# Gated attention written out straight, with one-piece evictions of the query and key projection and DMAs that place its halves

## The reference, cut to what matters

```
dist = softmax(mean(x @ Wr + br, axis=1))        # a gate picks 4 of 16 heads for each batch entry
_, idx = top_k(dist, 4)
Q, K, V = (x @ Wq + bq), (x @ Wk + bk), (x @ Wv + bv)     # split into heads of 64
Qs, Ks, Vs = gather(Q), gather(K), gather(V)     # only the 4 picked heads
score = softmax(einsum('bhqd,bhkd->bhqk', Qs, Ks) / 8, axis=-1)
O = einsum('bhqk,bhkd->bhqd', score, Vs)
x = x + (O.reshape(b, s, 256) @ Wo + bo)
```

## Time and profile before

| | us |
|---|---|
| median of 3 runs | 757.16 (755.01 to 757.79) |
| the profiled execution's own time | 755.7 |
| its span | 753.6 |
| gated attention, first scores to output projection | 219.0 to 454.7 |
| PE busy in the whole span | 590.0 (78%) |
| DVE busy | 514.2 (68%) |
| ACT busy | 314.8 (42%) |
| POOL busy | 334.3 (44%) |

### The profile page before, as it was taken

The page is one execution under the profiler, slowest core; times in us unless marked ns, Lnnn a source line. Parts: engine busy times, 40 slices in busy tenths (PEclk is TensorE's granted clock), DMA queues, the critical chain, the costliest instruction groups (busy, mean ns, idle before and its releaser), DMA issues. The chain is left out here.

```text
span 753.6 us, 12641 instructions
## 1 busy us (share of the span) xinstructions
PE 590.0 (78%) x3566; PEld 488.8 (65%) x3567; DVE 514.2 (68%) x980; ACT 314.8 (42%) x577; POOL 334.3 (44%) x296
## 2 busy tenths in 40 slices
PE   5588999952588999998998988677203989989985
PEld 4467888851457777776776777347202877867874
DVE  4698888857139888888888876476612556567562
ACT  2144555412158878788787770233101112112120
POOL 4344444534025344444444431134461196599144
PEclk9799999985699999999999999885556999999998
DMA  6121112000210000000000000762426025034000
GB/s 208 29 56 29 30 28 54 3 8 0 85 32 1 1 1 1 2 0 0 0 0 0 0 1 0 271 199 79 199 100 205 15 96 217 14 158 154 28 14 3
DMA packets 21039, 43.76 MB, mean 58 GB/s; under 512 B 2874, under 2 KB 14139, under 8 KB 18954
## 3 DMA queue, kind: packets, MB, share of 16 engines
q1 hardware_dynamic: 17130, 37.06, 14.8%
q0 software_dynamic: 1776, 4.23, 1.6%
q10 hardware_dynamic: 2096, 2.05, 0.9%
HBM read 31.58 MB, written 8.21 MB: 53 GB/s over the span
## 5 line engine op out<-in xcount | busy, mean ns | idle before, releaser
L889 POOL TENSOR_SCALAR h_p<-h_p,h_rs 128x1024 f32<-128x1024 f32 x64 | 72.1, 1127 | 123.1 <-DVE h_rs L1007 120.5
L1016 DVE TENSOR_REDUCE h_nmx<-h_psS 128x1 f32<-128x1024 f32 x64 | 78.0, 1219 | 20.9 <-PE h_psS L1103 20.2
L957 ACT ACTIVATE h_p<-h_psS,h_nmx 128x1024 f32<-128x1024 f32 x64 | 71.7, 1120 | 29.0 <-DVE h_nmx L1016 28.6
L994 DVE TENSOR_TENSOR h_pTl<-h_psT,h_pTh 128x512 fp32r<-128x512 f32 x128 | 81.3, 676 | 2.1 <-ACT h_pTh L932 2.1
L1066 PE MATMUL h_psT<-ident,h_p 128*128 128x128 f32 x512 | 71.6, 277 | 12.5 <-DVE h_pTl L994 12.3
L1066 PEld LDWEIGHTS h_psT<-ident,h_p 128*128 128x128 f32 x512 | 57.3, 140 | 30.9 <-DVE h_pTl L994 17.8
L932 ACT CAST h_pTh<-h_psT 128x512 fp32r<-128x512 f32 x128 | 69.8, 590 | 7.5 <-PE h_psT L1066 6.7
L1077 PE MATMUL h_psO<-h_pTh,h_vs 128*128 128x256 f32 x256 | 68.0, 301 | 4.6 <-DVE h_oT L1001 4.2
L308 POOL TENSOR_TENSOR a_p<-a_p,a_rs 128x616 f32<-128x616 f32 x32 | 39.0, 1219 | 73.4 <-DVE a_rs L355 73.4
L1077 PE MATMUL h_psO<-h_pTl,h_vs 128*128 128x256 f32 x256 | 62.1, 279 | 0.0
L1103 PE MATMUL h_psS<-h_kh,h_qs 128*128 128x512 f32 x128 | 57.0, 446 | 2.8 <-ACT h_p L957 2.4
(11 more groups left out here) (269 smaller groups left out, 1512.7 us busy)
## 6 DMA issues: line engine op xcount, KB each, us to landing
wst<-in_m_w SPq DMA_DIRECT2D x16, 1024.0 KB, 6.1
bias<-in_m_b SPq DMA_DIRECT2D x8, 640.0 KB, 8.2
rows<-c_blank SPq DMA_DIRECT2D x1, 3250.0 KB, 18.6
xg<-rows SPq DMA_DIRECT2D x1, 2990.0 KB, 11.5
a_qs<-a_qhi SPq DMA_DIRECT2D x16, 128.0 KB, 2.3
a_qs<-a_qlo SPq DMA_DIRECT2D x16, 128.0 KB, 2.3
x_all<-in_x SPq DMA_DIRECT2D x2, 768.0 KB, 10.7
whead<-in_f_w ACTq DMA_DIRECT2D x4, 192.0 KB, 3.8
```

The source lines that it names most:

```text
L889: pool.tensor_scalar(pr[:, c % 4], pr[:, c % 4], rs[:, c:c + 1], 0.0, ALU.mult, ALU.add).then_inc(pn_ready, 1)
L957: act.activation(pr[:, c % 4], psS[c % 2][:], ACT.Exp, bias=nmx[:, c:c + 1], scale=1.0, accum_out=sm[:, c:c + 1]).then_inc(exp_done, 1)
L994: vec.tensor_tensor(pTl[c // QP % 2][part], psT[hf][:], pTh[c // QP % 2][part], ALU.subtract).then_inc(pT_lo, 1)
L1016: vec.tensor_reduce(nmx[:, c:c + 1], psS[c % 2][:], AX.X, ALU.max, negate=True).then_inc(max_ready, 1)
```

## The change

- The loop is gone: all 64 units are written out, and `upto` is a plain wait on a constant. No ninth head is prepared.
- The weights of a head are read by PE straight from `whead`; POOL scales the query part of four heads at once (`scale_q(b)`), before the first unit.
- ACT evicts a projection in one instruction of 128 partitions into a new tile `hi`, and DVE forms the low part in one instruction into `lo`. Six DMAs of 64 x 512 from SP put the halves of `hi` and `lo` where `qs`, `kh` and `kl` want them (`qk_in` counts them). POOL's `duplicate` is gone.
- A projection is now four pieces on PE, each one matmul of 256 columns with one half of the contraction. In the units of a group of four (q % 4 = 0, 1, 2, 3) PE does none, piece 0 (behind the value step), pieces 1 and 2 (before and behind the value step), and piece 3 (between scores and transposes). A projection is done a half head earlier than before: during the first four units of head i the second half of head i + 1, during the last four the first half of head i + 2. Projection 2 (head 1, first half) comes before the first unit.
- ACT's part is in q = 3 and 7, DVE's in the next q = 4 and 0, there between `low` and `output`.

```diff
+            for p in range(2 * NI):                                # SP
+                i, ch = divmod(p, 2)
+                cols = slice(ch * CW, (ch + 1) * CW)
+                upto(sp, s_ps, NQ * (i - 1))
+                sp.wait_ge(qk_lo, p + 1)
+                low_half, high_half = slice(0, HD2), slice(HD2, P)
+                sp.dma_start(qs[i % 2][low_half, cols].bitcast(F32), hi[ch][low_half].bitcast(F32)).then_inc(qk_in[ch], 16)
...
-            def duplicate(n, c, par, ch):                          # POOL
...
-                pool.tensor_scalar(kh[par][0:HD2, cols], kh[par][HD2:P, cols], 1.0, 0.0, ALU.mult, ALU.add)
-                pool.tensor_scalar(kl[par][0:HD2, cols], kl[par][HD2:P, cols], 1.0, 0.0, ALU.mult,
-                                   ALU.add).then_inc(qk_ready, 1)
+            def scale_q(b):
+                pool.wait_ge(t["w_head"][b], 16 * NA)
+                w = whead[:, b * NA:(b + 1) * NA, :, 0:HD2].rearrange("p a k c -> p (a k) c")
+                pool.tensor_scalar(w, w, HD2 ** -0.5, 0.0, ALU.mult, ALU.add).then_inc(scaled, 1)
...
-                act.activation(qs[par][0:HD2, cols], ps[0:HD2], ACT.Identity, bias=bias[0], scale=1.0)
-                act.activation(kh[par][HD2:P, cols], ps[HD2:P], ACT.Identity, bias=bias[1],
+                upto(act, qk_in[p % 2], MOVES * (p // 2))
+                act.activation(hi[p % 2][:], ps[:], ACT.Identity, bias=bqk[:, p // 2:p // 2 + 1],
                                scale=1.0).then_inc(qk_hi, 1)
...
-                vec.scalar_tensor_tensor(qs[par][HD2:P, cols], ps[0:HD2], bias[0], qs[par][0:HD2, cols],
-                                         ALU.add, ALU.subtract)
-                vec.scalar_tensor_tensor(kl[par][HD2:P, cols], ps[HD2:P], bias[1], kh[par][HD2:P, cols],
+                vec.scalar_tensor_tensor(lo[p % 2][:], ps[:], bqk[:, p // 2:p // 2 + 1], hi[p % 2][:],
                                          ALU.add, ALU.subtract).then_inc(qk_lo, 1)
...
+            def project(p, piece, ps=psP):                         # PE
+                i, ch = divmod(p, 2)
+                hf, k = divmod(piece, KD)
+                if piece == 0:
+                    pe.wait_ge(scaled, i // NA + 1)
+                    if ps is psP:
+                        upto(pe, qk_lo, p)
+                cols, at = slice(hf * CW // 2, (hf + 1) * CW // 2), i // NA * S + ch * CW
+                ins = pe.matmul(ps[:, cols], whead[:, i, k, 0:2 * HD2], xnT[:, k, at + cols.start:at + cols.stop],
+                                start=(k == 0), stop=(k == KD - 1))
...
+                if q == 0:
+                    for c in range(2):
+                        pe.wait_ge(qk_in[c], MOVES * (i + 1))
```

More of the change, by code:

```diff
@@ L881, in _ @@
[L881 to L894, removed]
@@ L897, in _ @@
+            scale_q(0)
+            scale_q(1)
+            split_v(0)
+            for u in range(NU):
+                i, q = divmod(u, NQ)
+                pool.wait_ge(rs_ready, u + 1)
+                pool.tensor_scalar(pr[:, u % 4], pr[:, u % 4], rs[:, u:u + 1], 0.0, ALU.mult,
+                                   ALU.add).then_inc(pn_ready, 1)
+                if q == 6 and i + 1 < NI:
+                    split_v(i + 1)
             pool.memset(mhalf[:], -0.5).then_inc(half_ready, 1)
@@ L947, in _ @@
                 if i == 0:
[L948 to L975, removed]
+                    split_v(0)
+            for u in range(NU):
+                i, q = divmod(u, NQ)
+                if u >= LAG:
+                    high(u - LAG)
+                act.wait_ge(max_ready, u + 1)
+                upto(act, pT_ps, 2 * (u - 3))
+                act.activation(pr[:, u % 4], psS[u % 2][:], ACT.Exp, bias=nmx[:, u:u + 1], scale=1.0,
+                               accum_out=sm[:, u:u + 1]).then_inc(exp_done, 1)
+                if u % 2 == 0 and u >= 6:
+                    output((u - 6) // 2)
+                if u == 0:
+                    project(2)
+                if q in (3, 7) and 2 * i + 3 + q // 7 < 2 * NI:
+                    project(2 * i + 3 + q // 7)
+                if q == 5 and i + 1 < NI:
+                    split_v(i + 1)
+            high(NU - 3)
+            output(NG - 3)
+            high(NU - 2)
+            high(NU - 1)
+            output(NG - 2)
+            output(NG - 1)
         @block.vector
@@ new lines, in invert @@
+            def invert(u):
+                vec.wait_ge(exp_done, u + 1)
+                vec.reciprocal(rs[:, u:u + 1], sm[:, u:u + 1]).then_inc(rs_ready, 1)
+            project(0)
+            project(1, psO)
+            for u in range(NU):
+                i, q = divmod(u, NQ)
+                vec.wait_ge(s_ps, u + 1)
+                vec.tensor_reduce(nmx[:, u:u + 1], psS[u % 2][:], AX.X, ALU.max, negate=True).then_inc(max_ready, 1)
+                if u >= 1:
+                    invert(u - 1)
+                if u >= LAG:
+                    low(u - LAG)
+                if u == 1:
+                    project(2)
+                if q in (4, 0) and u > 0 and 2 * i + 2 + q // 4 < 2 * NI:
+                    project(2 * i + 2 + q // 4)
+                if u % 2 == 0 and u >= 6:
+                    output((u - 6) // 2)
@@ L1035, in _ @@
+            invert(NU - 1)
+            low(NU - 3)
+            output(NG - 3)
+            low(NU - 2)
+            low(NU - 1)
+            output(NG - 2)
+            output(NG - 1)
             for r in range(T // 2):
@@ L1080, in values @@
                     ins.then_inc(o_ps, 1)
-            project(0, 0, 0, 0)
-            project(0, 0, 0, 1, psO)
+            for p, ps in ((0, psP), (1, psO)):
+                for piece in range(2 * KD):
+                    project(p, piece, ps)
             pe.wait_ge(t["w_head"][1], 16 * NA)
@@ L1113, in _ @@
[L1113 to L1122 removed]
+            for u in range(NU):
+                i, q = divmod(u, NQ)
+                if q == 0:
+                    for c in range(2):
+                        pe.wait_ge(qk_in[c], MOVES * (i + 1))
+                upto(pe, exp_done, u - 1)
+                for hf in range(2):
+                    for part in (kh, kl):
+                        ins = pe.matmul(psS[u % 2][:, hf * CW:(hf + 1) * CW], qs[i % 2][:, q * P:(q + 1) * P],
+                                        part[i % 2][:, hf * CW:(hf + 1) * CW], start=(part is kh), stop=(part is kl))
+                ins.then_inc(s_ps, 1)
+                ahead = 2 * i + 3 + q // 4
+                if ahead >= 2 * NI:
+                    ahead = None
+                if ahead and q % 4 == 3:
+                    project(ahead, 3)
+                if u >= LAG:
+                    transposes(u - LAG)
+                if ahead and q % 4 == 2:
+                    project(ahead, 1)
+                if u >= 5:
+                    values((u - 5) // 2, (u - 5) % 2)
+                if ahead and q % 4 == 1:
+                    project(ahead, 0)
+                if ahead and q % 4 == 2:
+                    project(ahead, 2)
```

215 lines of the change are left out of this document (69 added, 146 removed).

## The result

The changed kernel takes 738.25 us (median of 4 runs, 737.68 to 740.46) against 756.09 before: a ratio of 0.977 (95% interval 0.9751 to 0.9789), 17.8 us faster. The forecast was 735.6, with a range of 727 to 748. The profiled execution took 740.46, with a span of 738.7.

A forecast was written before the change was run, and what follows sets the result against it. PE's and DVE's long blocks, in different units, were taken to make each other wait once a period. Terms -20.3 - 1.7 + 0.4 = -21.6 on 755.7 gave 734.1; the median's 1.5 made 735.6, range 727 to 748.

The forecast's parts named there:

- the middle of the stretch: Units 4 to 60: 12 periods of 13.12 and two without projection at 11.6, 180.6 against 200.9, so -20.3 us.
- The period: Four units on PE: 4 x 2.71 + 1.72 + 0.56 = 13.1; bounds 12.6 without the stall, 13.9 if DVE's instruction cost 1.55.
- Rival 1: PE's value step does not wait for `output`: periods 12.6, 10.84 without projection, so 728 us; chance 0.10.
- Rival 3: The gap moves: values held back more, q = 2 transposes wait again, periods 14.3; 754 us, within 0.5%; chance 0.07.
- Rival 4: The six DMAs land late, 4.5 too late before each of seven heads: +31.5, so 767 us, slower; chance 0.05.
- Rival 2: DVE's whole eviction is not cheaper, 1.55: period 13.9, +9.4, so 745 us; chance 0.14, or part of it.
- ACT likewise loses one of two: ACT's eviction drops one of two instructions; with 1.14 idle before its exponential, claimed worth nothing by itself.
- the start: Up to unit 4's scores: first scores at 221.0, not 219.03, partly recovered; net +0.4 us, bounds -1.5 and +2.0.
- The moves: Six DMAs per projection: issues 2.5 plus landing 2.3 is 4.8 against 8.7 of cover; hidden, 3.9 to spare.
- The loop: Removing the loop's branches and register waits: at most 14 x 0.06 = 0.8 us, counted in the sum.

## Why the prediction was right

The mechanism held: with one instruction in place of two on DVE and ACT, PE's wait for the low parts went, and the middle of the stretch gained 19.5 of the 20.3 forecast for it. From the last copy to the output projection the kernel gained 18.7 of the 21.6 forecast, and 17.8 by the medians.

*The period.* Replayed: 13.12 with a projection, 11.6 without; measured: 13.12 and 23.59/2 = 11.8. The whole-height instruction on DVE was taken at 0.76 from the rows of `low` and measured 0.74. A piece was 0.43, the four additional loads cost nothing. PE's wait for `pTl` went, and one for `oT` came, forecast at 0.56, measured 0.32. That the period agrees to 0.01 is partly luck: this wait was 0.24 shorter, but a unit without stall took 301.86 - 299.11 = 2.75, not 2.71, which is 0.16 in four, and about half of the periods are 13.18 in place of 13.05. Nor is the projection in front of `output` by itself the reason for the wait, as the prediction has it: with `output` in front the wait stays, since `olo` comes as late.

*The rivals.* Rival 1, PE's floor of 12.6, was not reached, since the 0.32 for `olo` stayed and DVE's order did not free it. Rival 3 did not occur: transposes waited for `pTl` once, 0.5, from 229 to 420. Rival 4 appeared only with eight more moves a projection. Rival 2 gave 13.9 for a DVE instruction of 1.55; the experiment with just that gave 13.94.

*What failed: "ACT likewise loses one of two; it has idle time, so that is worth nothing by itself."* In this arrangement it is worth as much as DVE's: halved again, ACT's alone cost 11.1, DVE's alone 10.8 and both 20.9. ACT's idle time lies ahead of exponentials in other units. In the unit with q = 3 the eviction stands between an exponential and the copies for which DVE's `low` waits, and these, the projection and the output step are one chain to PE's value step. The total did not suffer from this error, because the replay ran with ACT in time, which was so only as ACT's eviction was short. That was luck.

*What was mis-sized: the start.* "It comes back in part ... +0.4" was +3.4. I had replayed scores and exponentials, but not piece 0 of projection 3, which stands on PE between the scores of units 1 and 2 and waits for DVE's low part of projection 2, that in turn waits for ACT's eviction behind the exponential of unit 0: 3.09 us with all of PE's list behind it. The first scores themselves came 1.6 later from the last copy (14.38 against 12.74), where 2.0 was forecast; from there to the scores of unit 4 it took 1.8 more in place of 1.6 less. Moving projection 2's evictions forward removed it (22.14); so, in part, did moving projection 3 back (23.23).

*The moves.* Forecast at 0.42 an issue with 3.9 to spare; they issue every 0.64 (0.60 long), land in 2.4 and have about 2.4 to spare (13.05 less 4.4 until the low part is ready, six issues of 0.64 and the landing). Hidden as forecast, but with 0.67 of wait at head 0, where I had seen 1.7 of room.

*The loop.* At most 0.8 was forecast; the whole time shows none, the trace up to 1.7.

## What to carry to other kernels

Replay one period with the engines' fixed orders, and each cross-engine wait in it, before pricing an edit: an instruction on an engine that idles elsewhere can cost its full length if it stands in front of what the critical chain waits for. Replay the first units as well, with every instruction that a moved step puts between them. And before reordering two steps of which one waits for another engine, see whether the other one fills that wait.

## What the runs showed of the hardware

An operation on 128 partitions took as long as on 64 of the same columns: 0.74 against 0.74 to 0.76 on DVE, 0.70 against 0.68 on ACT. On SP, these DMAs of 64 x 512 between tiles in SBUF took 0.60 each and issued every 0.64 in a row, where the loads from HBM just before them took 0.35 to 0.42.

PE's granted clock fell in the start of the changed kernel, behind its wait of 3.09. Busy time by stretch, 226.00 to 232.00, columns as in the earlier trace rows, in the changed kernel:

```profile
226.00:232.00 6.00, 4.53 (x13) 3.69 (x14) 2.20 (x4) 1.97 (x4) 1.32 (x2) 0.72 0.38 88
```

and with projection 2's evictions moved forward:

```profile
226.00:232.00 6.00, 5.64 (x30) 4.56 (x30) 4.08 (x9) 4.39 (x9) 3.38 (x3) 1.00 0.37 84
```

In this stretch the fall lies right behind the wait:

```profile
227.40:230.20 2.80, 2.73 (x7) 2.19 (x8) 0.00 (x0) 0.23 (x2) 0.00 (x0) 0.50 0.42 96
```

That is the lower of the clock's two levels, 1.2 GHz. There the score matmuls of unit 2 stand 0.43 apart (229.31 to 229.74 above) in place of 0.23 in unit 0. From piece 0 at 227.47 to the next pieces at 230.16 PE took 2.69, where 0.43 + 4 x 0.23 = 1.35 would do at the upper level. So the wait of 3 us cost about another 1.3, and both went with one edit. The run with eight more DMAs shows it behind some of its waits and not behind others: its unit 16 took 5.27 at 0.50, and its unit 8 took 2.82 at 1.00.
